# Second attention layer: values made once and reloaded with rows repeated, and sums over a head's rows taken in four column groups

## The reference

```
Q, K, V = x @ WQ, x @ WK, x @ WV        # 16 heads x 8; Q and K are rotated by position
QKD     = (Q K^T) * scale_h ** (i - j)  for j <= i     # scale_h = 1 - 2**(-5-h)
R       = QKD V ;  R normalized over each head's 8 columns ;  y = R @ WO
```

## Time and profile before

| | |
|---|---|
| median of 3 runs | 1274.31 us (1266.7, 1274.31, 1274.86) |
| the profiled execution | 1260.86 us, span 1259.1 us |
| mean granted TensorE clock | 0.930 of full speed |
| TensorE busy (matmul records) | 1128.0 us, 90% of the span |
| VectorE, ScalarE, GpSimd busy | 902.0, 697.0, 510.6 us (72%, 55%, 41%) |

### The profile page before, as it was taken

The page is one execution under the profiler, slowest core; times in us unless marked ns, Lnnn a source line. Parts: engine busy times, 40 slices in busy tenths (PEclk is TensorE's granted clock), DMA queues, the critical chain, the costliest instruction groups (busy, mean ns, idle before and its releaser), DMA issues.

```text
span 1259.1 us, 15646 instructions
## 1 busy us (share of the span) xinstructions
PE 1128.0 (90%) x5494; PEld 714.2 (57%) x5494; DVE 902.0 (72%) x2074; ACT 697.0 (55%) x1167; POOL 510.6 (41%) x482
## 2 busy tenths in 40 slices
PE   7999999899999999999999776899998978639977
PEld 6765544355445574655544323597776746318967
DVE  4856437556658857779799998685688799956554
ACT  4575666876735755745676544653424777425221
POOL 2322123212225220065238455663276366584372
PEclk8999999999999879999999875898999989659999
DMA  8500000000000000000000000425323302046673
GB/s 266 194 1 1 1 1 0 1 1 1 1 17 1 1 1 1 18 1 1 1 1 1 0 0 17 149 87 180 126 82 101 109 16 97 16 127 217 236 254 118
DMA packets 39838, 76.86 MB, mean 61 GB/s; under 512 B 3281, under 2 KB 29009, under 8 KB 39249
## 3 DMA queue, kind: packets, MB, share of 16 engines
q0 software_dynamic: 10688, 51.39, 11.9%
q1 hardware_dynamic: 29072, 24.48, 6.1%
HBM read 65.30 MB, written 10.55 MB: 60 GB/s over the span
## 4 chain that ended last, share of the span: by engine, by line
PE 55%; DVE 13%; ACT 11%; POOL 10%; issue 6%; DMA 5%; POOLq 0%; SPq 0%; DVEq 0%; ACTq 0%
PE ps L894 7%; PE ps L2161 5%; PE ps L1469 4%; PE ps L2169 3%; PE ps L1278 2%; DVE own L2027 2%; PE ps L1287 2%; PE ps L668 2%; DMA g_f<-w,slot 2%; PE ps L856 2%; POOL sx L2414 2%; POOL own L2051 2%; PE ps L654 2%; POOL own L2446 1%; PE ps L1589 1%
## 5 line engine op out<-in xcount | busy, mean ns | idle before, releaser
L894 PE MATMUL ps<-own,g_f 128*128 128x512 f32 x320 | 146.1, 597 | 1.1 <-DVE own L1103 1.1
L1221 POOL TENSOR_TENSOR own<-own 128x512 f32<-128x512 f32 x32 | 43.4, 1355 | 162.4 <-PE ps L894 92.1
L894 PEld LDWEIGHTS ps<-own,g_f 128*128 128x128 f32 x320 | 59.1, 191 | 66.8 <-issue 58.4
L2027 DVE TENSOR_TENSOR_SCAN own<-own,carry 128x512 f32<-128x512 f32 x48 | 77.2, 1608 | 20.4 <-POOL own L2051 17.1
L2051 POOL TENSOR_TENSOR own<-own 128x512 f32<-128x512 f32 x32 | 51.9, 1622 | 77.6 <-ACT own L1977 77.6
L1931 PE MATMUL ps<-own,g_c 128*128 128x512 f32 x64 | 45.2, 795 | 40.7 <-POOL own L2057 40.5
L2238 ACT ACTIVATE own<-ps 128x512 f32<-128x512 f32 x60 | 35.7, 596 | 79.6 <-PE ps L2161 79.0
L1968 ACT ACTIVATE own<-own,Acol 128x512 f32<-128x512 f32 x64 | 45.2, 714 | 56.4 <-PE ps L1931 56.2
L2352 DVE TENSOR_TENSOR own<-ps,own 128x512 f32<-128x512 f32 x60 | 41.1, 684 | 47.1 <-PE ps L2161 40.2
L526 ACT ACTIVATE own<-xs,sm 128x128 f32<-128x128 f32 x128 | 52.5, 482 | 31.1 <-POOL sm L518 31.0
L1887 POOL TENSOR_TENSOR own<-own 128x512 f32<-128x512 f32 x32 | 43.6, 1365 | 55.4 <-DVE own L1861 51.7
(11 more groups left out here) (480 smaller groups left out, 3095.3 us busy)
## 6 DMA issues: line engine op xcount, KB each, us to landing
sx<-brow SPq DMA_DIRECT2D x4, 960.0 KB, 10.4
so<-own SPq DMA_DIRECT2D x11, 256.0 KB, 5.0
own<-sx SPq DMA_DIRECT2D x10, 256.0 KB, 4.8
g_l<-p_l SPq DMA_DIRECT2D x1, 2449.0 KB, 13.6
g_f<-p_f SPq DMA_DIRECT2D x1, 2223.5 KB, 9.1
own<-cs SPq DMA_DIRECT2D x8, 256.0 KB, 3.0
g_l<-p_l SPq DMA_DIRECT2D x1, 1866.0 KB, 10.9
g_l<-t_wmod SPq DMA_DIRECT2D x1, 1152.0 KB, 10.3
```

Source lines behind the costliest of these rows:

```text
L894: x = e.matmul(s.bank["V%d%d%d" % (it, k, cc)][:, :], ew2[:, m, 128 * cc:128 * cc + 128], gm, start=False, stop=m == 3)
L1221: e.tensor_tensor(R.gm[m % 2], R.g[m], R.mask[k][m], ALU.mult).then_inc(*s.pool.up("m%d%d%d" % (it, k, m)))
L2027: e.tensor_tensor_scan(H, A, H, init, ALU.mult, ALU.add).then_inc(*s.dve.up("H%d" % n))
```

## The change

V is now made once per chunk (one product with the 128 columns `wv2`), copied by ScalarE to tile 10, stored by SyncE to a DRAM buffer `sv[c]`, and read back eight times: load n takes the 16 rows of value column n and writes each to 8 partitions. The eight loads fill eight tiles (`KV` has eight entries now); loads 3 to 7 wait for the finished Q, because their tiles are in use before. Both multiplications by K, on VectorE for even and GpSimd for odd n, now read a tile and write it in place.

The products with `ind` are replaced: for g = 0 and 1, four products, one for each of states 4g to 4g+3, with the 128x32 stationary `ind2` and the state's whole 512 columns moving, each to its own 32 partitions of one bank `S{g}`. ScalarE copies the bank to a tile, TensorE transposes it in four blocks (bank `R{g}`), and VectorE reduces and subtracts the mean in two halves. The decay is spread to a 128x512 tile once. Bank `R` is no longer held.

```diff
 ORDER = (
...
+        decays = sb("decays", [128, W])
+        wv2 = sb("wv2", [128, 128])
+        ind2 = sb("ind2", [128, 32])
+        sv = [nc.dram_tensor(f"sv{c}", (128, W), F32, kind="Internal").ap() for c in range(NC)]
...
 (p4_vector)
+            e.tensor_copy(wv2[:, :].rearrange("p (h n) -> p h n", h=16), V["wvr"].rearrange("p (n h d) -> p h n d", n=8, d=8)[:, :, :, 0]).then_inc(*P.dve.up("wv2"))
+            e.memset(ind2[:, 16:32], 0.0)
+            e.tensor_copy(ind2[:, 0:16], V["ind"]).then_inc(*P.dve.up("ind2"))
+            yield
+            q.wait_ge(landed["decay"], 16)
+            e.tensor_copy(decays[:, :], decay[:, :].broadcast_to([128, W])).then_inc(*P.dve.up("decays"))
...
 (l2a_sync)
+            q.wait_ge(*s.act("v"))
+            e.dma_start(sv[c], T[c][10]).then_inc(d_v2[c], 16)
+            for n in range(8):
+                yield
+                q.wait_ge(d_v2[c], 16)
+                if n >= 3:
+                    q.wait_ge(*s.dve("qT"))
+                rows = sv[c].rearrange("(h n) t -> n h t", n=8)[n]
+                e.dma_start(T[c][KV[n]], rows.unsqueeze(1).broadcast_to([16, 8, W])).then_inc(d_kv[c][n], 16)
-        KV = (5, 7, 8, 9)
+        KV = (8, 9, 10, 5, 7, 2, 3, 1)
 (l2a_tensor)
+            p = banks.take(s, q, "v", (s.act, "v"))
+            e.matmul(p[:, :], wv2[:, :], h, start=True, stop=True).then_inc(*s.pe.up("v"))
             for n in ("wk", "wks", "wq", "wqs"):
...
-            R = banks.hold(s, q, "R", (s.dve, "xc"))
-            for n in range(10):
-                if n < 8:
-                    yield
-                    p = banks.take(s, q, "v%d" % n, (s.act if n % 2 else s.dve, "v%d" % n))
-                    e.matmul(p[:, :], V["wvr"][:, 128 * n:128 * n + 128], h, start=True, stop=True).then_inc(*s.pe.up("v%d" % n))
-                if n >= 2:
-                    yield
-                    q.wait_ge(*s.pool("q%d" % (n - 2)))
-                    for i in range(4):
-                        m = e.matmul(tl(R, i).rearrange("p (h e) -> p h e", e=8)[:, :, n - 2], tl(T[c][KV[(n - 2) % 4]], i), V["ind"], start=True, stop=True)
-                    m.then_inc(*s.pe.up("R%d" % (n - 2)))
-            banks.back(s, "R")
+            for g in range(2):
+                yield
+                p = banks.take(s, q, "S%d" % g, (s.act, "S%d" % g))
+                for n in range(4 * g, 4 * g + 4):
+                    q.wait_ge(*s.pool("q%d" % n))
+                for j in range(4):
+                    m = e.matmul(p[32 * j:32 * j + 32, :], ind2[:, :], T[c][KV[4 * g + j]], start=True, stop=True)
+                m.then_inc(*s.pe.up("S%d" % g))
+            for g in range(2):
+                yield
+                p = banks.take(s, q, "R%d" % g, (s.dve, "xc%d" % g))
+                q.wait_ge(*s.act("S%d" % g))
+                for i in range(4):
+                    m = e.transpose(tl(p, i), tl(T[c][KV[g]], i), V["ident"])
+                m.then_inc(*s.pe.up("R%d" % g))
 (l2a_scalar)
+            q.wait_ge(*s.pe("v"))
+            e.activation(T[c][10], s.bank["v"][:, :], ACT.Copy).then_inc(*s.act.up("v"))
...
-                    e.activation(T[c][KV[n % 4]], s.bank["v%d" % n][:, :], ACT.Copy).then_inc(*s.act.up("v%d" % n))
...
+                if n in (5, 9):
+                    g = n // 9
+                    yield
+                    q.wait_ge(*s.pe("S%d" % g))
+                    e.activation(T[c][KV[g]], s.bank["S%d" % g][:, :], ACT.Copy).then_inc(*s.act.up("S%d" % g))
 (l2a_vector)
-                        e.tensor_tensor(kv, s.bank["v%d" % n][:, :], T[c][4], ALU.mult).then_inc(*s.dve.up("v%d" % n))
+                        q.wait_ge(*s.dve("kT"))
+                        q.wait_ge(d_kv[c][n], 16)
+                        e.tensor_tensor(kv, kv, T[c][4], ALU.mult).then_inc(*s.dve.up("v%d" % n))
...
-                    e.tensor_tensor_scan(kv, decay.broadcast_to([128, W]), kv, init, ALU.mult, ALU.add).then_inc(*s.dve.up("scan%d" % n))
+                    e.tensor_tensor_scan(kv, decays[:, :], kv, init, ALU.mult, ALU.add).then_inc(*s.dve.up("scan%d" % n))
-            e.tensor_reduce(nm, R3, AX.X, ALU.add).then_inc(*s.dve.up("sum"))
+            for g, half in ((0, vs), (1, nm)):
+                yield
+                q.wait_ge(*s.pe("R%d" % g))
+                e.tensor_reduce(half.rearrange("p (i h) -> p i h", i=4), R3[g], AX.X, ALU.add).then_inc(*s.dve.up("sum%d" % g))
+            e.tensor_tensor(nm, nm, vs, ALU.add).then_inc(*s.dve.up("sum"))
...
-            e.tensor_tensor(x3, R3, nm.unsqueeze(2).broadcast_to([128, 64, 8]), ALU.add).then_inc(*s.dve.up("xc"))
+            for g in range(2):
+                e.tensor_tensor(x4[:, :, :, 4 * g:4 * g + 4], R3[g], nm.rearrange("p (i h) -> p i h", i=4).unsqueeze(3).broadcast_to([128, 4, 16, 4]), ALU.add).then_inc(*s.dve.up("xc%d" % g))
 (l2a_gpsimd, odd n)
-                    q.wait_ge(*s.act("v%d" % n))
+                    q.wait_ge(d_kv[c][n], 16)
                     q.wait_ge(*s.dve("kT"))
                     e.tensor_tensor(kv, kv, T[c][4], ALU.mult).then_inc(*s.pool.up("kv%d" % n))
```

More of the change, by code:

```diff
@@ new lines @@
+    "mclmbcmkclccdhhmiclcclhmmmkhlhccmbhmcckpcpcdpphhcnfncgejjymddhadrndfnbbbmggngakpaapfadmaffnfaankfninkmakrarffkfddkfrrdnb"
+    "bblnlaalakkkbkkbhlibbgalallbfgtdfffbnlbbflgglfaaabkbdgkbbngblnnnackabhfpkaallallfgblkfdggakiakddkdfekaafkbbakgbaotbdaoak"
+    "lgaapoiqakiolaalpafaaflfqqakfdpkfdkaaiqqgkkdpdinddinndnadndfndbddnidngndidifddifidddfndnidkdkkdkddikindkkddidnnndinniian"
+    "afdanfnafaafdfiaddkdikdkdikpaaaddfikafaafdfanisfanqlfbbbqgbggbgngnlaalsfslalaslsipaaafaaaffkbbfbbkgakkgkgaapkgklllbblklb"
@@ new lines @@
+    "bagggggfpbfbbbafaaafaafkaglbplaaklklgqbllaklblbkbfbkbllglfgkdfbbbbpbglfbifqbbgklbkkgqbbkbbbkglgkgkbqkgllbbblafalaqfafaag"
+    "fagakgkkfgakrrchkcclkpchhlpclhhppccflcpmcllhlhabbmfmbgmmgmbgahhkbbakbgmffmmgamlmccflfalaflqfbbbfkfffckfackbhkhhhfbbhfbhk"
+    "fbgmmcgcmlccggcgmcchmchmrcgcmhcmccbbhmhamgfmafacfccfffcfmarafkfkkkfcckfaakkfkchmaccccchrhahmfcfmafmafkhmffkkfcckrfafmfak"
+    "kkkcraahafakkafhfkafbffkbfkfkakhagqfbbbgbkbbkhgagmammbmmllbbkmlmqalbkkkkklalcfqchlalckhchccgbgbchkhbgbmbbkgmppmmbrlppgfq"
@@ L72 @@
+    "cmmmmmsmmmmnrdlidlilldidndilninssnrrvndiiinrrdidndrsidnsnwchwwwchchndiiindicdnsccddhnichccnschdnndidmimcicncirhcnscmnscc"
+    "ihcnrdismmcrmdmccnhdcnncnccrsmschmcmmssccricchdirccmhmswdcnncniccmrhcnnncnnmrdmmccncnhncnncnchnrmccnnssccnhrmscnwnsnndmi"
+    "dcniccrsmmhndimddidcncnndimdimwddiddnccnnchndimcmdiddidccncdhmcnncsndimmwdiddisxxddnnndirndiddddinnxnddnssddissdddddimms"
+    "nnnsmmiddddindnsndddinsnnmidddddsndddnxniinnnddddddwinnnsdddddinndddddindnddddindndnindndndnnnnnx"
 )
@@ L249, in build @@
         d_cs = [sem(f"d_cs{c}") for c in range(NC)]
+        d_v2 = [sem(f"d_v{c}") for c in range(NC)]
+        d_kv = [[sem(f"d_k{c}{i}") for i in range(8)] for c in range(NC)]
         d_sent = [sem(f"d_s{c}") for c in range(NC)]
@@ L1644, in l2a_vector @@
                 if n < 8:
-                    kv = T[c][KV[n % 4]]
+                    kv = T[c][KV[n]]
                     if n % 2:
@@ L1661, in l2a_vector @@
                         init = carry2[:, c - 1, n:n + 1]
-                    q.wait_ge(landed["decay"], 16)
-                    e.tensor_tensor_scan(kv, decay.broadcast_to([128, W]), kv, init, ALU.mult, ALU.add).then_inc(*s.dve.up("scan%d" % n))
+                    q.wait_ge(*P.dve("decays"))
+                    e.tensor_tensor_scan(kv, decays[:, :], kv, init, ALU.mult, ALU.add).then_inc(*s.dve.up("scan%d" % n))
             nm, vs = z[:, 490:554], z[:, 554:618]
-            R3 = s.bank["R"][:, :].rearrange("p (g n) -> p g n", n=8)
+            R3 = [s.bank["R%d" % g][:, :].rearrange("p (i j h) -> p i h j", i=4, j=4)[:, :, 0:16, :] for g in range(2)]
+            for g, half in ((0, vs), (1, nm)):
+                yield
+                q.wait_ge(*s.pe("R%d" % g))
+                e.tensor_reduce(half.rearrange("p (i h) -> p i h", i=4), R3[g], AX.X, ALU.add).then_inc(*s.dve.up("sum%d" % g))
             yield
-            q.wait_ge(*s.pe("R7"))
-            e.tensor_reduce(nm, R3, AX.X, ALU.add).then_inc(*s.dve.up("sum"))
+            q.wait_ge(*s.dve.now())
+            e.tensor_tensor(nm, nm, vs, ALU.add).then_inc(*s.dve.up("sum"))
             yield
```

83 lines of the change are left out of this document (32 added, 51 removed).

## The result

The kernel after takes 1298.4 us (median of 4 runs, 1293.8 to 1300.4) against 1271.2 us of the kernel before in the same session: a ratio of 1.0229, interval 1.0178 to 1.0281. So it is slower; whether by more than 2% the interval leaves open. I had forecast 1255 us and a range of 1228 to 1280; the prediction was wrong, in sign as well.

A forecast was written before the change was run, and what follows sets the result against it. TensorE, busy 90% of the span, was taken as the bound. Products -19.2, waits and queues -2, loads +1, VectorE's share +1: about -19 us, from a median of 1274.3 to 1255 us; range 1228 to 1280.

The forecast's parts named there:

- main term: Second attention's value and indicator products on TensorE: 27.1 us on the chain, 71% of it goes, 19.2 us gained.
- rival B: Sum products' column groups run one behind the other: 8.4 us come off, 1.6 lost again, 1267 us; chance 0.13.
- Rival A: All 39 us of spared TensorE time come off, as the new order fills the time: 1235 us; chance 0.2.
- its granted clock falls: Sign of being wrong: TensorE's granted clock, 0.86 already in the first stretch, falls and lengthens all that stays; no size.
- counted at 1 us: V's store and loads leave 6.3 us open per chunk, 25 us in all; other chunks' work fills it, 1 us lost.
- Rival D: Value loads come late at each chunk's scans: 6.3 us each, 25 us, slower at 1290 us; chance 0.13.
- D's second mark: Long waits on SyncE for L3F's rows ahead of chunk 2's value loads; 10 us was priced there.
- priced at 0: The order written anew for all layers: worth 0, with 8 us either way.
- contention term: VectorE's 16 even multiplications with two SBUF inputs beside GpSimd: 2.6 us more, under 1 us on the chain.
- The decay tile: The scan's full decay tile in place of a column: worth nothing, median 1284 ns either way.
- The copies of S: ScalarE's copies between sums and transposes: part of 1.3 us later per chunk, covered by other chunks; 5 us if uncovered.
- V's way: Copy, store and load of V per chunk: 10.4 us against 0.6 before; sign in the trace 6 to 11 us.

The follow-up runs named there:

- e12: Kernel before, value products cut to 16 columns and one indicator product of four left per set, nothing added: 1261.3 us, 0.9937 of the kernel before.
- e2: Kernel before in its old order, with only the sums in four column groups, their copies and transposes; no value loads: 1258.2 us, 1.0032 of the kernel before.
- e14: e2's operations (column-group sums, no value loads) in e11's mixed order: 1274.3 us, 1.0136 of the kernel before.
- e6: e1 with seven useless TensorE products per chunk put back, 24 us of work in all: 1286.2 us, 1.0138 of the kernel before.
- e5: e1 with all eight value loads of chunk 2 behind chunk 0's L3F row loads on SyncE: 1292.1 us, 1.0144 of the kernel before.
- e1: All new operations of the kernel after, in the order string of the kernel before: 1275.3 us, 1.0168 of the kernel before.
- e3: Kernel before in its old order, with only the values made once and loaded back; sums as before: 1271.0 us, 1.0158 of the kernel before.
- e7: e1 with the value loads reading cosine table rows, so not depending on V's product or store: 1280.5 us, 1.0073 of the kernel before.
- e8: e1 with each value load moving 64 of its 512 columns: 1286.1 us, 1.0159 of the kernel before.
- e18: Rerun: all new operations in e11's mixed order, value loads reading cosine table rows without waiting for V's store: 1281.6 us, 1.0110 of the kernel before.
- e16: e11 run again, all new operations in the mixed order: 1281.4 us, 1.0101 of the kernel before.
- e17: e5 run again, all new operations in the old order: 1295.5 us, 1.0219 of the kernel before.
- e9: The kernel after run again with no edit: 1296.4 us, 1.0223 of the kernel before.
- e10: Kernel after with the old order up to chunk 0 of the second attention, new order from there: 1289.2 us, 1.0169 of the kernel before.
- e11: Kernel after with the mixed order, old up to chunk 2 of the second attention and new behind it: 1275.2 us, 1.0028 of the kernel before.
- e13: Kernel before with VectorE's 16 even multiplications reading another SBUF tile in place of the PSUM bank: 1255.3 us, 0.9998 of the kernel before.
- e4: Kernel after with the scan reading the decay column in place of the full tile: 1291.8 us, 1.0312 of the kernel before.

## Why the prediction was wrong

**The main term failed: "27.1 us on the chain, 71% of their time goes".** The sizes of the operations were right: at full clock a set S is 1.07 us for the 1.15 that I took, and the column groups do overlap, so rival B is out (the 1.6 us that it loses again I had worked out nowhere). What was wrong is turning a share of the chain into time. e12 takes the two lines' work away and adds nothing, and 8.0 us come off (interval 4.8 to 11.3) where the term, sized for e12, said 15 to 27. The chain of waits names one engine at each step, the last, and not how late the next one is. VectorE's and GpSimd's work in these stretches, 182 and 118 us, stays as it is, and in e12 it took over the places of TensorE's on the chain. Rival A, all 39 us, is out with it. TensorE at 95% of a stretch did not bound that stretch.

**The clock, a mark that I had named and not priced.** I wrote that I should be wrong "if its granted clock falls". It fell in the kernel after. The two levels are full and half, so a mean of 0.930 over 1259.1 us is 176 us at the lower level, and 0.904 over 1298.6 is 249 us: 73 us more. Of the 38.9 us of work that I counted out, the busy time shows 5.3 us; the other 33.6 us are about what 73 us more at half the rate add, by this estimate up to 36 us. In steps of 2 us, the fall in the second stretch, and the two pieces of TensorE's timeline that begin behind its longest and its last idle time before it:

```profile
576.00:578.00 2.00, 1.26 (x8) 0.43 (x8) 1.89 (x4) 1.97 (x3) 0.00 (x0) 1.00 0.00 0
578.00:580.00 2.00, 1.78 (x10) 1.78 (x10) 2.00 (x5) 1.97 (x4) 0.16 (x1) 0.63 0.00 0
580.00:582.00 2.00, 2.00 (x12) 2.00 (x11) 2.00 (x3) 1.99 (x3) 1.42 (x1) 0.50 0.00 0
...
545.98 1.98 PE L906 MATMUL ps<-own,g_f 128*128 128x512 f32 x4 [3.40 <-DVE own L1115]
...
578.22 1.82 PE L1290 MATMUL ps<-own 128*128 128x128 f32 x8 [0.96 <-DVE early L1121]
```

The Trainium skill, page "TensorE: Matmul & The Clock Gate", section "Why this matters for your kernels", has a rule that idle gaps between bursts bring the half rate back. The trace agrees only in part: the low clock comes behind 40 us in which TensorE was busy for 30, but the longest gap there, 3.40 us, left the clock at 1.00, and it fell behind one of 0.96 us. What the low clock costs in time is not shown either, and it is not needed for the loss of the gain: e2 gains nothing and e14 loses 1.4% at the clock of the kernel before, and e12's clock explains at most 4 us. e6, as fast as e5 with a higher clock and 24 us more work, can be read either way.

**The loads were counted at 1 us and cost some 17 to 20 in the old order.** e1 less e2 is 1.0168 - 1.0032 = 0.0136 of 1256 us, and e3 against the kernel before is 0.0158; the spared TensorE time is already in both. Rival D had the price (25 us) about right, with a chance of 0.13, but the runs do not bear out its mechanism. The sentence that failed is "other chunks fill them as long as they have ready work, which 95% of TensorE says they do": 95% of TensorE says nothing on whether VectorE and GpSimd, which wait for the values, have other work. But the waits for the loads are not most of the loss: the kernel after, which loses the most, has 5.4 us of them. e7, which has none, gives back about half of the old order's loss by its figures, and the intervals overlap; e8 cuts them to 0.7 us of GpSimd and shows no gain; e18 against e16 takes an 11.2 us wait away for nothing. D's second mark, SyncE held ahead of chunk 2, is seen in e17 (9.3 us of VectorE), but e1 without it is about as slow, and in the kernel after, where the fourth load of chunk 2 is issued 18.5 us behind the first, no engine waits for it. In the mixed order all new operations take 1.0028 and 1.0101 where the sums alone take 1.0136, so there the loads cost nothing that can be measured. What else the new way of V costs in the old order, and why an order changes it, stays open.

**The order was priced at 0, with 8 us either way.** Against the old one, for the new operations, that holds as a whole (e9 beside e17). Its parts are larger: up to chunk 0 it costs perhaps 7 us (e10 against e9), from there up to chunk 2 another 9 to 14 us (1.0101 and 1.0028 against 1.0169), and its last part gives some 15 us back against the old one (1.2% in both pairs, e5 and e11, e17 and e16), but only where the loads are: for the sums alone it costs 1% (e14). In the packed stretch it fills VectorE and leaves TensorE idle.

**The contention term** of 2.6 us came out as 5.2 us on the multiplications (16.0 us busy for 10.8, a mean of 1.00 us where I had named 0.75 to 0.95 as the sign), and the scans took 6.6 us more (58.7 for 52.1). The first comes from the operand: e13, with the operand alone, has 15.6 us. It costs no time there. The second comes for the most part from the packing: in e17 the scan's median with a carry is 1284 ns again, and all scans are busy for 53.9 us. The decay tile is worth nothing, as forecast (e4). The copies of S on ScalarE cost nothing measurable (e2).

The forecast of V's way, 6 to 11 us, was right at the median (7). The store takes 2.0 us where I went by 5.0 of another store. The Trainium skill's page "DMA: Bandwidth & Descriptors", Anatomy of one DMA, fits its 2.6 us for 256 KB to transfers that GpSimd issues, which I had not said, and these are SyncE's; it was nearer for the store, and too low for the loads (4.7, up to 13.3).

## What to carry to other kernels

A share of the chain of waits is no estimate of what an engine's work is worth: here it said 15 to 27 us, and 8 came off. Before counting on it, take the work away in place (smaller operands, same waits) and time that: one experiment of e12's kind would have told that some 39 us of TensorE are worth 8. Ask of a wait that a change adds which engine stands behind it and whether that engine has other work, not whether the busiest one has; and look whether the kernel before waited there as well. Busy time by itself can mislead in the same way: in the kernel after TensorE's is nearly unchanged, because the rest of its work ran at the lower clock for longer. And do not change order and operations together where either can be timed alone: here each changes what the other costs.

## What the runs showed of the hardware

Four float32 products of 32 output partitions and 512 columns, each with its own moving data, take 1.07 us together at a granted clock of 1.00 and 1.94 at 0.50; their records are 0.59 to 1.06 us each. A load that repeats each of 16 rows over 8 partitions (256 KB) lands in 3.5 to 14.5 us in e17, and with an eighth of the bytes in 2.4 at the median. The even multiplication with two SBUF inputs takes up to 1.75 us in e13, and with one in PSUM never over 0.69 in the kernel before. With seven TensorE products of no use put into each chunk the mean granted clock was 0.918 over four runs, against 0.908 and 0.914 in e5 and e1, and no time was lost beyond the noise.
